# Transposes interleaved with bf16 products, and x transposed two tiles ahead, in a routed expert layer

## The reference, cut to what matters

```python
# x, ctx: (8, 256, 256); 8 experts, 2 per token, hidden 512, rank-16 factors on every expert matrix
x = x + tanh(g_xattn) * retention(layernorm(x), ctx, ctx, Wq, Wk, Wv)       # gated cross attention, with decay mask
xf = layernorm(x).reshape(2048, 256)
scores = softmax(xf @ Wg.T); weights, experts = top_k(scores, 2)            # weights divided by their sum
h1 = xf @ W1[e].T + (xf @ A1[e].T) @ B1[e].T + b1[e]                        # for each expert e
h3 = xf @ W3[e].T + (xf @ A3[e].T) @ B3[e].T + b3[e]
g  = silu(h1) * h3
y  = g @ W2[e].T + (g @ A2[e].T) @ B2[e].T + b2[e]
x = x + tanh(g_ffn) * sum_e gate[e] * y[e]
```

## Time and profile before

| | |
|---|---|
| median of 3 runs | 330.47 us (330.36 to 336.72) |
| profiled execution, span from first to last instruction | 325.4 us |
| profiled execution, its own time | not listed; the median is 5.1 us above the span |
| PE busy / DVE / ACT / POOL | 297.9 / 248.2 / 206.0 / 210.8 us |
| mean granted TensorE clock | 0.975 |
| first part of the program | 0 to about 118 us |
| 39 tiles | about 118 to 316 us, last scatter issued at 317.14 us |

### The profile page before, as it was taken

The page is one execution under the profiler, slowest core; times in us unless marked ns, Lnnn a source line. Parts: engine busy times, 40 slices in busy tenths (PEclk is TensorE's granted clock), DMA queues, the critical chain, the costliest instruction groups (busy, mean ns, idle before and its releaser), DMA issues. The chain is left out here.

```text
span 325.4 us, 7435 instructions
## 1 busy us (share of the span) xinstructions
PE 297.9 (92%) x1755; PEld 230.0 (71%) x1755; DVE 248.2 (76%) x607; ACT 206.0 (63%) x486; POOL 210.8 (65%) x246
## 2 busy tenths in 40 slices
PE   7589989999997798999999999999999999999960
PEld 3468778788886656776777777777777777777740
DVE  2679879889999998697988976767776776777750
ACT  5635755766878577787675565665675665675550
POOL 2457878888893098866756656766577776666241
PEclk9799999999999699999999999999999999999996
DMA  7968997999972169567747675766533223333100
GB/s 265 391 158 240 280 297 253 294 279 278 278 244 85 17 225 296 138 201 200 205 139 206 175 187 186 175 187 197 148 56 55 52 51 66 53 45 61 20 0 0
DMA packets 30424, 54.35 MB, mean 167 GB/s; under 512 B 7232, under 2 KB 15808, under 8 KB 30112
## 3 DMA queue, kind: packets, MB, share of 16 engines
q1 hardware_dynamic: 14672, 36.10, 34.1%
q0 software_dynamic: 7488, 9.36, 16.7%
q10 hardware_dynamic: 8224, 8.42, 8.6%
HBM read 41.92 MB, written 10.65 MB: 162 GB/s over the span
## 5 line engine op out<-in xcount | busy, mean ns | idle before, releaser
L1079 POOL DMA_INDIRECT out<-ys,cols x39 | 64.7, 1660 | 58.4 <-DMA out<-ys,cols 33.0
L883 ACT ACTIVATE gh<-bank 128x512 fp32r<-128x512 f32 x39 | 23.4, 599 | 61.0 <-PE bank L648 61.0
L640 PE MATMUL bank<-WH,xh 128*128 x156 | 55.7, 438 | 0.1
L1056 POOL DMA_INDIRECT xg<-xn_rows,colg x39 | 40.0, 1026 | 20.5 <-POOL colg L1034 10.3
L992 POOL TENSOR_TENSOR WL<-stage,WH 128x512 bf16<-128x512 f32 x38 | 47.9, 1278 | 7.3 <-ACT WH L752 7.1
L640 PE MATMUL bank<-WH,xl 128*128 x156 | 49.0, 395 | 0.0
L640 PE MATMUL bank<-WL,xb 128*128 x156 | 47.2, 385 | 0.0
L752 ACT ACTIVATE WH<-stage 128x512 fp32r<-128x512 f32 x38 | 22.9, 628 | 17.7 <-DVE stage L1110 14.5
L640 PEld LDWEIGHTS bank<-WH,xl 128*128 128x128 f32 x156 | 29.2, 188 | 6.8 <-DVE xl L1493 0.4
L1497 DVE TENSOR_TENSOR gl<-bank,gh 128x512 fp32r<-128x512 f32 x39 | 26.9, 689 | 8.8 <-ACT gh L883 8.7
L657 PE MATMUL bank<-WH,gh 128*128 x156 | 32.0, 327 | 1.5 <-ACT gh L883 1.5
(11 more groups left out here) (229 smaller groups left out, 702.2 us busy)
## 6 DMA issues: line engine op xcount, KB each, us to landing
BB<-biases_in SPq DMA_DIRECT2D x16, 640.0 KB, 4.1
stage<-w_all_in SPq DMA_DIRECT2D x38, 256.0 KB, 5.1
BA<-biases_in SPq DMA_DIRECT2D x8, 640.0 KB, 3.9
WL<-w_all_in SPq DMA_DIRECT2D x10, 256.0 KB, 4.7
LS<-WH SPq DMA_DIRECT2D x45, 48.0 KB
xn_rows<-xn ACTq DMA_DIRECT2D x8, 256.0 KB, 4.1
out<-x ACTq DMA_DIRECT2D x7, 256.0 KB, 3.1
cx<-ctxT_in ACTq DMA_DIRECT2D x6, 256.0 KB, 6.5
```

The lines of the kernel that those rows point to most:

```text
L640: last = nc.tensor.matmul(dst[:, :], lhs[p][:, c * P:(c + 1) * P], W[:, bass.ds(e * (UNITS * UC) + (2 * kind + c) * UC, HID)], start=(part ...
L883: nc.scalar.activation(gh[:], pG[:, :], ACT.Copy).then_inc(s_gh, 1)
L1056: nc.gpsimd.indirect_dma_start(out=xg[q][:], out_offset=None, in_=xn2_d[0:JA * P, :] if i < NA else xn2_d, in_offset=bass.IndirectOffsetOn ...
L1079: nc.gpsimd.indirect_dma_start(out=out_rows, out_offset=bass.IndirectOffsetOnAxis(ap=cols[:, i:i + 1], axis=0), in_=ys[p][:], in_offset=No ...
```

## The change

On PE the transposes no longer stand in a row. The four of g (tile i-1) stand each in front of one of the four bf16 products of tile i: the two last of the first projection and, since the second projection now adds its `xb` terms first, the two first of the second. The two of x stand in front of the first two bf16 products of `down`, and they are those of tile i+2 (from i = 1 on); in tiles 0 and 1 the transposes of x of tile i+1 stand in the first projection, ahead of its `xb` terms. ACT does `x_parts(i+1)` ahead of `g_high(i-1)`, and DVE does `x_rest(i+1)` at the head of the tile, ahead of `beside_h1(i)`.

```diff
-            def x_transposes(i, q):
+            def x_ready(i, q):
                 pe.wait_ge(s_xg[q], 16 * ((i - q) // XBUF + 1))
                 if i > 0:
                     pe.wait_ge(s_xh, i)
                     pe.wait_ge(s_xb, i)
                     pe.wait_ge(s_xl, i)
...
+            def up_first(i, p, e, first, late_x):
+
+                pos_wait(pe, s_h1b, i)
+                pe.wait_ge(s_xh, i + 1)
+                up(pH1, xh, WH, p, e, 0, 0, start=True)
+                up(pH1, xh, WH, p, e, 0, 1)
+                pe.wait_ge(s_xl, i + 1)
+                up(pH1, xl, WH, p, e, 0, 0)
+                up(pH1, xl, WH, p, e, 0, 1)
+                pe.wait_ge(s_xb, i + 1)
+                if late_x:
+                    x_transposes(i + 1, (i + 1) % XBUF)
+                if not first:
+                    g_transpose(i - 1, 0)
+                up(pH1, xb, WL, p, e, 0, 0)
+                if not first:
+                    g_transpose(i - 1, 1)
+                up(pH1, xb, WL, p, e, 0, 1, stop=True).then_inc(s_h1, 1)
+
+            def up_second(i, p, e, first):
+
+                pos_wait(pe, s_h3b, i)
+                if not first:
+                    g_transpose(i - 1, 2)
+                up(pH3, xb, WL, p, e, 1, 0, start=True)
+                if not first:
+                    g_transpose(i - 1, 3)
+                up(pH3, xb, WL, p, e, 1, 1)
+                up(pH3, xh, WH, p, e, 1, 0)
+                up(pH3, xh, WH, p, e, 1, 1)
+                up(pH3, xl, WH, p, e, 1, 0)
+                up(pH3, xl, WH, p, e, 1, 1, stop=True).then_inc(s_h3, 1)
...
+                pe.wait_ge(s_gb, i + 1)
+                if x_next is not None:
+                    x_ready(x_next, x_next % XBUF)
+                for c in range(HC):
+                    if x_next is not None and c < CH:
+                        x_transpose(x_next % XBUF, c)
+                    last = product(gb, WL, c, stop=(c == HC - 1))
                 last.then_inc(s_y, 1)
...
-                    down(i - 1, expert((q - 1) % XBUF))
+                    down(i - 1, expert((q - 1) % XBUF), i + 2 if i + 2 < NT_SLOTS else None)
...
@@ (ACT tile)
+                if more:
+                    x_parts(i + 1, 1 - p)
                 if not first:
                     g_high(i - 1)
-                if more:
-                    x_parts(i + 1, 1 - p)
...
@@ (DVE tile)
+                if more:
+                    x_rest(i + 1, 1 - p)
                 beside_h1(i)
...
                     g_rest(i - 1)
-                if more:
-                    x_rest(i + 1, 1 - p)
                 beside_h3(i)
```

More of the change, by code:

```diff
@@ L628, in x_transposes @@
                     pe.wait_ge(s_xl, i)
-                for c in range(CH):
[L630 to L643, removed]
@@ L645, in g_transposes, with x_transpose @@
-            def g_transposes(i):
-                pe.wait_ge(s_g, i + 1)
-                for c in range(HC):
[L648 to L659, removed]
+            def x_transpose(q, c):
+                last = nc.tensor.transpose(pX[:, c * P:(c + 1) * P], xg[q][:, c * P:(c + 1) * P], ident[:])
+                if c == CH - 1:
+                    last.then_inc(s_xT, 1)
@@ new lines, in x_transposes, with g_transpose, up @@
+            def x_transposes(i, q):
+                x_ready(i, q)
+                for c in range(CH):
+                    x_transpose(q, c)
+            def g_transpose(i, c):
+                if c == 0:
+                    pe.wait_ge(s_g, i + 1)
+                last = nc.tensor.transpose(pG[:, c * P:(c + 1) * P], g[:, c * P:(c + 1) * P], ident[:])
+                if c == HC - 1:
+                    last.then_inc(s_gT, 1)
+            def up(dst, lhs, W, p, e, kind, c, start=False, stop=False):
+                return nc.tensor.matmul(dst[:, :], lhs[p][:, c * P:(c + 1) * P],
+                                        W[:, bass.ds(e * (UNITS * UC) + (2 * kind + c) * UC, HID)], start=start, stop=stop)
@@ new lines, in down, with product @@
+            def down(i, e, x_next):
+                def product(lhs, W, c, start=False, stop=False):
+                    return nc.tensor.matmul(pY[:, 0:D], lhs[:, c * P:(c + 1) * P],
+                                            W[:, bass.ds(e * (UNITS * UC) + 4 * UC + c * D, D)], start=start, stop=stop)
+                pos_wait(pe, s_ys, i)
+                pe.wait_ge(s_gh, i + 1)
+                for c in range(HC):
+                    product(gh, WH, c, start=(c == 0))
+                pe.wait_ge(s_gl, i + 1)
+                for c in range(HC):
+                    product(gl, WH, c)
+                pe.wait_ge(s_gb, i + 1)
+                if x_next is not None:
+                    x_ready(x_next, x_next % XBUF)
+                for c in range(HC):
+                    if x_next is not None and c < CH:
+                        x_transpose(x_next % XBUF, c)
+                    last = product(gb, WL, c, stop=(c == HC - 1))
@@ L674, in tile @@
                 p = q % 2
-                up(pH1, i, p, expert(q), 0, s_h1)
-                if not first:
-                    g_transposes(i - 1)
-                if more:
-                    x_transposes(i + 1, (q + 1) % XBUF)
+                up_first(i, p, expert(q), first, i < 2)
                 if first:
                     pe.wait_ge(s_wl, (E - 2) * UNITS + 4)
-                up(pH3, i, p, expert(q), 1, s_h3)
+                up_second(i, p, expert(q), first)
                 if more:
@@ L718, in _ @@
             tile_steps(pe, tile)
-            g_transposes(NT_SLOTS - 1)
-            down(NT_SLOTS - 1, expert((NT_SLOTS - 1) % XBUF))
+            for c in range(HC):
+                g_transpose(NT_SLOTS - 1, c)
+            down(NT_SLOTS - 1, expert((NT_SLOTS - 1) % XBUF), None)
         @block.scalar
```

## The result

The changed kernel takes 335.41 us (median of 4 runs, 333.62 to 336.56) where the kernel before, run beside it, takes 331.10: a ratio of 1.0139, with a 95% interval of 1.0092 to 1.0186. So it is 1.0 to 1.4% slower, less than the 2% that count as a change; 334.9 us had been forecast. The ratios leave out executions over 1.5% above the fastest of their kernel, and the traces of e1 (341.1 us) and e8 (341.7 us) are of such ones and serve here only for single waits, steps and the clock.

What follows compares the result with a forecast made beforehand. PE bounds a quiet tile at 4.82 us, with scatters following about as slowly up to 253 us. Quiet tiles 0, DVE's waits +5.1, fewer late gathers and scatters -0.7: +4.4 on 330.5 gives 334.9 us, 8-in-10 range 329 to 338.5.

Steps and rivals of the forecast that it cites:

- A transpose in front of a bf16 product costs 0.11: PE's interleaved transposes: each still takes 0.11 us start to start, as in a row, so six gain 0 a tile.
- Rivals 1 and 4: 1: covered transposes last 0.055, 330 us, chance 0.14; 4: short transposes, scatters pulling together, 323 us, chance 0.04.
- Rival 2: ACT makes x parts in time, so DVE's waits hide but gathers' do not: 332.5 us, chance 0.12.
- A quiet tile costs the same: Loop's quiet tiles: small gain of 0.03 cancelled by late gl; 0 change, bounds -0.04 and +0.05 a tile.
- the chain from g to down: From g's last transpose to down: gh and gl products both just meet, gl late by 0 to 0.05 us.
- DVE's new head, +5.1: x_rest at DVE's tile head delays h1 add and gl, so PE waits in tiles 0 to 12: +5.1 us.
- Less met of late gathers and scatters, -0.7: PE, being later, no longer meets today's few late gathers and scatters: -0.7 us, an estimate (0 to -1).
- The gather one tile earlier adds nothing to that: x wanted 2.4 us sooner would cost 1.4 to 2.5 us once, but does not add to the 4.4.
- 5.1 lies around it: Gap between the profiled span forecast, 329.8 us, and the forecast median, 334.9 us.
- The clock does not fall: PE's clock row stays unchanged in the profile of the changed kernel.
- Rival 3: PE's gaps in tiles 1 and 5 make the clock fall: 338 us, two falls 341; chance 0.12.
- The reading of the earlier trace: Prediction had the clock's digit fall to 6 in the slice ending at 122 us, behind idle PE.

Runs made afterwards that it cites:

- e1: Changed kernel with DVE's old order alone (xl of the next tile behind gl again): ratio 1.0200 to the kernel before.
- e8: Changed kernel with only 64 columns of g as weights of each g transpose, leaving out half of g's values: ratio 1.0120 to the kernel before.
- e6: Changed kernel with g's four transposes in a row again and the second projection's old order; x still two tiles ahead: ratio 1.0233 to the kernel before.
- e3: Changed kernel with the old orders of both ACT and DVE, leaving PE's part of the change: ratio 1.0284 to the kernel before.
- e5: Changed kernel with x one tile ahead as before and old orders of ACT and DVE; g's transposes stay interleaved: ratio 1.0247 to the kernel before.
- e4: Changed kernel with DVE's old order in tiles 0 to 12 and its new order from tile 13 on: ratio 1.0215 to the kernel before.
- e7: Changed kernel with DVE's other work of tiles 3 to 12 (routing of the last batches) behind gl: ratio 1.0149 to the kernel before.
- e9: Changed kernel run once more, unaltered, in six more runs: 335.50 us, ratio 1.0102 to the kernel before.
- e10: Changed kernel with each x gather from tile 6 on issued one step earlier, ahead of a scatter: ratio 1.0196 to the kernel before.
- e11: The kernel before, with x gathers issued one step earlier, ahead of a scatter: ratio 1.0080 to the unaltered kernel before.
- e2: Changed kernel with ACT's old order alone (gh ahead of the x parts): ratio 1.2432 to the kernel before.

## Why the prediction was right, and where it was not

- **A transpose in front of a bf16 product costs 0.11**: right, in every trace, and e8 shows that covering the load could not have shortened it. Rivals 1 and 4 are out. Rival 2 (DVE's waits hide) is out too: PE waits 3.7 us for `gl`, the same in both traces of the changed kernel.
- **A quiet tile costs the same**: right in sum (4.82 against 4.83). Two terms of 0.04 cancel: e6 holds the one, and its difference to the whole change is the other. The step that was incomplete is the chain from g to down: it followed `gh` and `gl` and left out `gb`, whose 0.84 us to the next tile was nearly at its limit; ACT's new order gives 0.36 of room there (1.24 against 0.88). Without it a tile costs 0.17 to 0.28 more (e3, e5).
- **DVE's new head, +5.1**: the waits came where they were forecast. In tile 0 the bias add was put at 122.0 and came at 122.73 less the 0.65 of a later start; in tile 5 from a free ACT to `gl` 3.25 was worked out and 150.47 to 153.72 is 3.25. By tile: 1.2 (forecast 1.0), 0.8 (1.2), 0.6 (0.5), 0.7 (1.1), 1.4 (0.9), 0.6 (0.4), in sum 5.3 against 5.1. Single tiles are off by up to 0.5, so that the sums agree to 0.2 is partly luck. But as the price of DVE's order it was wrong: e1 and e4 undo it and win nothing, e7 moves the other work and wins nothing. The 5 us are what this place takes as long as it is the latest; x gathers, a halved clock, late `g` and, in e1, late `xl` in quiet tiles stood behind it and took as much.
- **Less met of late gathers and scatters, -0.7**: 0.8 came back in tiles 16 and 19.
- **The gather one tile earlier adds nothing to that**: this step failed. The first trace bears it out, e9 does not: 2.3 us more of waits for x, 1.8 of them in tiles 4 and 21, where the first trace has none. The difference between the medians, 1.0102 to 1.0139, is 3.4 to 4.6 us, so it holds DVE's term and some of the gathers' and gives back a part that no single trace separates. That the forecast met the median to 0.5 us is partly luck: before's trace is of an execution 3 us shorter than the median, and "5.1 lies around it" should have been 1.9 and 3 us of chance.
- **The clock does not fall**: right for both traces of the changed kernel; its other executions left no trace. Rival 3's mechanism exists, and it is common: in the traces of e1, e3, e4, e7, e8, e10 and e11 the clock is half behind a gap among the tiles, once or twice, and each time 1.7 us are lost. The gaps were 1.68 to 2.46 us in one piece, or 1.30 and 1.12, or 1.26 and 0.53, close together; but it held behind 1.54 (e9), 1.67 (e8) and 1.72 (e4). DVE's wait in tile 0 shortened the gap in tile 1, but did not rule the fall out: e7 has the same tile 0 and lost the clock behind 1.68. The 1.5 us of e9 are close to that, so that neither trace of the changed kernel shows a fall is partly luck. The reading of the earlier trace rows was also wrong: the slice with the 6 is the fourteenth, which ends at 114 us and not at 122, ahead of the first tile.

What stays open: how the loss of the change divides between DVE's term, the gathers' and the clock's on average, since traces show single executions; why interleaving costs its 0.04; and whether the 0.84 us behind `gb` is the issue of the instructions there.

## What to carry to other kernels

A change that moves steps on three engines at once is not a sum of its parts: here every part alone, and the whole less one part, was at best as fast as all together (1.020 to 1.243 against 1.010 to 1.014). For the orders of ACT and DVE the traces show why: one makes up for the other's lateness (e2). Before crediting a wait with its length, ask what stands right behind it; in a loop with several chains near their limit, removing the latest one uncovers the next, and only a trace with it removed tells the price. And of work that depends on gathers, take more than one execution's trace before and after: here the waits for `gl` and `gh` repeated to a tenth of a us, waits for landings did not. Look at the granted clock behind each gap before you put a difference down to the edit: 1.7 us came or went with it here, in tiles whose program was the same.

## What was not expected of the hardware

- A float32 transpose of 128 columns takes 0.11 us start to start in front of a bf16 product, with weights of 128 and of 64 columns alike; float32 products of 8 columns with loads of 128 take 0.11 as well, bf16 ones of 64 columns 0.03.
- A product whose operands were ready started 0.84 to 0.88 us after the last operand of the products in front of it (e3, e5, before).
- The granted clock was halved, at a cost of 1.7 us, behind a single gap of 2.46 us in e1 and of 1.68 us in e7, though PE was busy throughout afterwards; behind 1.67 (e8) and 1.72 (e4) it held.
- The same gathers in the same order left waits for x between 1.1 and 3.4 us in two executions of one kernel.
